# Moving source-record scatters out of the first layer's edge pass: three beside each group instead of six

## What is computed

```python
# layer 0, graph attention (8 heads of 32)
h = (x @ W).reshape(n, H, C)
e = leaky(a_src[src] + a_dst[dst])
alpha = softmax of e over the edges of each dst
out = segment_sum(h[src] * alpha, dst) + bias
x = x + layer_norm(out + x_in) * ln_w + ln_b
# layer 0, mixture: 8 experts, top 2 of a router's softmax
x = x + combine(gelu(t @ w1[e] + b1[e]) @ w2[e] + b2[e])
# layer 1, messages: need h[src], h[dst] and the projected edge attributes
```

## Time and profile before

| | |
|---|---|
| median of the runs | 7105.77 us |
| profiled execution, span | 7405.0 us (the page gives its span, and no time around it) |
| busy, PE / DVE / POOL | 67% / 56% / 49% |
| edge pass of the first layer | about 790 to 2105 us |
| end of gat, to the next block | 2105 to 2187.6 us |
| router, to the next block | 2210 to 2267.6 us |
| first mixture, to the next block | 2267.6 to 2637.2 us |

### The profile page before, as it was taken

How to read it: one execution, slowest core, us unless ns; L and a number is a source line. 1 busy time by engine, 2 the same in 40 slices (tenths; PEclk the granted TensorE clock), 3 DMA queues, 4 the chain that set the end, 5 groups by cost and what they waited for, 6 DMA issues and landing times. The chain is left out here.

```text
span 7405.0 us, 83243 instructions
## 1 busy us (share of the span) xinstructions
PE 4987.3 (67%) x21442; PEld 3487.6 (47%) x21443; DVE 4140.2 (56%) x11930; ACT 2331.7 (31%) x4546; POOL 3609.5 (49%) x3179
## 2 busy tenths in 40 slices
PE   1995477777737966667783677639994555545685
PEld 1663365555525644445552555425662323223474
DVE  9202388888874667774525777773453334433534
ACT  0332244444411223332123555533322222211132
POOL 4777677777742327771034554300007673766043
PEclk9997678877758988888856777759996677766687
DMA  2553344434412255552132222200013332333324
GB/s 52 139 141 74 84 110 112 111 108 109 108 50 69 66 87 165 160 167 64 41 85 77 69 69 68 55 15 9 13 29 93 89 93 63 90 92 88 108 77 105
DMA packets 408552, 630.27 MB, mean 85 GB/s; under 512 B 163019, under 2 KB 290119, under 8 KB 406851
## 3 DMA queue, kind: packets, MB, share of 16 engines
q0 software_dynamic: 180096, 360.11, 18.7%
q1 hardware_dynamic: 227822, 260.35, 13.3%
q10 hardware_dynamic: 308, 6.40, 0.3%
HBM read 470.99 MB, written 154.65 MB: 84 GB/s over the span
## 5 line engine op out<-in xcount | busy, mean ns | idle before, releaser
L779 POOL DMA_INDIRECT conv_rows<-rows_b,index x832 | 843.4, 1014 | 1235.4 <-SPq L2682 884.5
L811 DVE TENSOR_TENSOR acc<-acc,ps 125x257 f32 (+1 forms) x1664 | 701.4, 422 | 930.5 <-DMA acc<-slots,ffn_slot_of 348.8
L2728 PE MATMUL ps<-conv_rows,conv_weight_of 128*125 128x256 f32 x1664 | 633.0, 520 | 599.1 <-issue 297.7
L332 POOL DMA_INDIRECT records_src<-by_src_edge_stage,by_src_edge_slot x400 | 560.0, 1400 | 458.0 <-DMA by_src_edge_stage<-edge_rows 340.4
L2728 PEld LDWEIGHTS ps<-conv_rows,conv_weight_of 128*125 128x125 f32 x1664 | 367.3, 248 | 864.8 <-issue 575.8
L779 POOL DMA_INDIRECT gat_rows<-rows,index x416 | 501.9, 1207 | 256.9 <-PE ps L1089 136.2
L779 POOL DMA_INDIRECT mpnn_rows<-rows_b,index x416 | 472.9, 1137 | 305.3 <-issue 122.1
L496 POOL DMA_INDIRECT records_dst<-front_back,front_dst_addr x400 | 503.6, 1259 | 234.7 <-issue 234.7
L779 POOL DMA_INDIRECT hyp_rows<-rows,index x416 | 417.1, 1003 | 407.8 <-PE ps L2335 274.3
L2716 ACT ACTIVATE conv_weight_of<-conv_onehot_b,index 128x125 f32<-128x125 bf16 x832 | 251.5, 386 | 980.2 <-DVE conv_onehot_b L2700 797.4
L1013 ACT CAST room<-ps 125x1024 bf16<-125x1024 f32 x416 | 409.0, 1016 | 458.3 <-PE ps L1076 374.8
(11 more groups left out here) (582 smaller groups left out, 10558.5 us busy)
## 6 DMA issues: line engine op xcount, KB each, us to landing
mpnn_edge<-records_src SPq DMA_DIRECT2D x104, 512.0 KB
edge_rows<-front_edge_ring SPq DMA_DIRECT2D x100, 451.5 KB
by_src_edge_stage<-edge_rows SPq DMA_DIRECT2D x100, 451.5 KB
conv_rows<-rows_b,index POOLq DMA_INDIRECT x832
front_attr<-in_edge_attr SPq DMA_DIRECT2D x100, 112.0 KB
rows_b<-acc SPq DMA_DIRECT2D x15, 560.0 KB
second_w<-in_L_ffn_w SPq DMA_DIRECT2D x1, 8192.0 KB
slots<-mlp_y SPq DMA_DIRECT2D x56, 128.0 KB
```

Source lines behind the costliest of these rows:

```text
L332: pool.indirect_dma_start(out=self.S.records["src"], out_offset=bass.IndirectOffsetOnAxis(ap=self.addr[:, c:c + 1], axis=0), in_=self.stag ...
L779: pool.indirect_dma_start(out=rows[:, n % U, t, :], out_offset=None, in_=table, in_offset=bass.IndirectOffsetOnAxis(ap=ends[:, n * G + t:n ...
L811: dve.tensor_tensor(here, here, S.ps[0:P, t % banks, 0:width], ALU.add).then_inc(added, 1)
L2728: pe.matmul(S.ps[0:P, t, 0:D], weight_of[:, q.slot, t, :], rows[:, q.slot, t, :], start=True, stop=True).then_inc(summed, 1)
```

## The change

The same 400 columns are scattered in the same order; their division over the four places goes from 312 + 24 + 28 + 36 to 156 + 48 + 40 + 156. In the mixture SP now issues the weights of an expert first and the edge loads behind them, and the loads begin with expert 1 and not with expert 2. The rule that divides the rest over the experts gives 20, 20, 20, 24, 24, 24 and 24 columns for experts 1 to 7, where it gave 4, 4, 4, 8, 8 and 8 for experts 2 to 7.

```diff
@@ gat
-                edges.load(sp, 6 * GROUPS)
+                edges.load(sp, 3 * GROUPS)
...
-                gather_groups(pool, ends, S.rows, rows, summed, gathered, go, lambda: edges.scatter(pool, 6))
+                gather_groups(pool, ends, S.rows, rows, summed, gathered, go, lambda: edges.scatter(pool, 3))
@@ gat, the end
-                edges.load(sp, 24)
+                edges.load(sp, 48)
...
-                edges.scatter(pool, 24)
+                edges.scatter(pool, 48)
@@ expert_weights
-                    edges.load(sp, 28)
+                    edges.load(sp, 40)
...
-                    edges.scatter(pool, 28)
+                    edges.scatter(pool, 40)
@@ experts
                     if e >= 2:
                         sp.wait_ge(done[h], e // 2)
-                        columns = edges.unloaded() // (steps - e)
-                        edges.load(sp, columns - columns % SG if e + 1 < steps else edges.unloaded())
                     sp.dma_start(w1[:, h], w_first(e)).then_inc(loaded[h], 16)
                     sp.dma_start(w2[:, h], w_last(e)).then_inc(loaded[h], 16)
                     if e == 0:
                         biases()
+                    if e >= 1:
+                        columns = edges.unloaded() // (steps - e)
+                        edges.load(sp, columns - columns % SG if e + 1 < steps else edges.unloaded())
```

## The result

The changed kernel takes 7151.47 us (median of 20 runs, 7094.45 to 7161.85), the kernel before 7106.95 us (20 runs, 7042.85 to 7117.21): ratio 1.0062 [1.0042, 1.0081], 44.5 us more. The forecast was 7148 us, same within 1%.

A forecast was written before the change was run, and what follows sets the result against it. DVE was taken to pace the edge pass, POOL to end gat and router last, PE to bound the mixture. Terms +35.8 + 17.9 - 10 - 1 = +42.7 us on 7105.8 gave 7148 us, range 7090 to 7195.

The forecast's parts named there:

- End of gat, +35.8 us: End of gat: 24 more scatters follow DVE's end, POOL is last, nothing hides them; 1.49 us each, +35.8 us.
- The upper end: End of gat: +39 us if each scatter costs the 1.327 + 0.3 us of the edge pass.
- Router, +17.9 us: Router block: 12 more scatters behind DVE's end, where POOL is last, at 1.49 us each, +17.9 us.
- Mixture, 0 us: Mixture: 120 more scatters hidden beside PE's experts, POOL landing before SP's last store; 0 us.
- rival 3: Mixture's tail: scatters above 1.64 us make POOL last, at 1.9 us each +13 us; 7178 us in all; chance 20%.
- The slack: Mixture's end: POOL's scatters land about 7 us before SP's last store, with landing at about 2.7 us.
- Edge pass, -10 us at the start and -1 in pace: Edge pass: fewer scatters shorten the start's burst, middle of 0 and -20 us; the steady pace, set by DVE, hardly changes.
- POOL's wait for PE, forecast at 390 us: Edge pass: POOL's wait for PE's sums grows about 5 us a group, from 136.2 to about 390 us.
- Rival 1: Edge pass: each of 51 periods loses 0.9 us and the start 20 us, giving 7094 us; chance 14%.
- Rival 2: End of gat: all 48 scatters fit beside DVE's operations, leaving the router's term and start's gain, 7113 us; chance 6%.

The follow-up runs named there:

- e_end48: Kernel before with 48 scatters instead of 24 at the end of gat, the 24 taken out of the mixture; 7533.60 us, ratio 1.0052.
- e_best: Kernel before with 16 scatters at the end of gat, 20 beside the router, 52 in the mixture with its new load order; 7457.38 us, ratio 0.9968.
- e_router40: Kernel before with 40 instead of 28 scatters beside the router, the mixture keeping 24; 7511.63 us, ratio 1.0020.
- e_mixorder: Kernel before with only the changed kernel's order of loads in the mixture's SP queue; 7490.99 us, ratio 1.0003.
- e_combo: Changed kernel with no scatters in first three groups, 4 in other 49, 16 at gat's end, 20 beside router, 168 in mixture; 7072.43 us, ratio 0.9954.
- e_pass3: Changed kernel with 24 scatters at the end of gat and 28 beside the router again, so 192 in the mixture; 7461.51 us, ratio 0.9947.
- e_none: Changed kernel with no scatters in the edge pass, 24 at the end of gat, 28 beside the router, 348 in the mixture; 7321.14 us.
- b_again: Kernel before with only an empty line added, for a second profile; 7492.18 us, ratio 1.0001.
- a_again: Changed kernel with only an empty line added, on the second chip; 7508.53 us, ratio 1.0037 to the kernel before.
- e_split: Changed kernel with each of five large DVE operations at the end of gat cut into 25 of 125x256; 7137.46 us, ratio 1.0045 to the kernel before.
- e_nofirst4: e_mixorder without scatters in the first four groups, 60 columns in the mixture; 7462.48 us, ratio 0.9963 to the kernel before.

## Why the prediction was right

**End of gat, +35.8 us.** Measured +35.4 in the changed kernel and +35.7 alone (e_end48). The reading that carried it was who ends last: POOL, 7 us behind DVE (10.3 us counted to the next block's start, e_best), so that each scatter added counts in full at 1.49 us. The upper end (+39, at the pace of the edge pass) was not needed.

**Router, +17.9 us.** +17.0, and +17.4 alone (e_router40). Right by the same reading.

**Mixture, 0 us.** -0.4 us, and e_mixorder shows that the order of SP's queue is free. POOL's pace over the last 50 issues was (2630.04 - 2554.43)/50 = 1.51 us, under the 1.64 of rival 3. The slack was 3.9 us, where the forecast had 7: landing took 4.2 us and not 2.7, and POOL's DRAIN of 2.8 us was not in the forecast at all; on the other side SP closed 4.7 us behind the start of its last store, to which the forecast had counted. That the slack is small but real is bracketed by 168 columns (e_combo, no loss) and 192 (e_pass3, 4 to 8 us lost, POOL last).

**Edge pass, -10 us at the start and -1 in pace.** Measured -9.0 by the second scaling and -0.8 behind it. The size was right by luck: its reason was not. The forecast took the middle between a stall that ends with the burst and one that does not, from a profile in which ACT waited 14.21 us for something outside the trace, and DVE 20.26 us for ACT. In the profiles at 7105 us, ACT has no such wait. The gain there is plain order in POOL's queue: the gathers of groups 2 to 4 stand behind fewer scatters. It is smaller than the 17.9 us of scatters taken out, because the second scaling cannot come much earlier: it is 64.9 us behind the first gather in the changed kernel, and still 62.4 with no scatter at all (e_none; 62.6 in e_combo). POOL's wait for PE, forecast at 390 us, was 321.9: it started from 97.3 on this chip and not from 136.2.

**Rival 1** (the pass gains) does not hold where the kernel runs at 7105 us: even with no scatters the period falls by 0.11 us only. It holds in part on the first two chips: start -13.5 us, period from the second scaling 24.49 to 24.05, 35.6 us in all (b_again to a_again; 10.0 us and 24.55 to 24.05 against e_mixorder), and the time grew by 25 us and not by 44. It was weighed at 0.9 us a group; half of that was there.

**Rival 2** (hidden at the end of gat) is excluded by e_end48. By the rule of the Trainium skill (SBUF — State Buffer, "Who interferes with whom") that it rested on, `tensor_tensor` of two SBUF inputs would not hold POOL's descriptor generation. The trace of the changed kernel disagrees once more (11.41 us beside L1155), and e_split narrows it: a single long operation holds it to its end, and 25 short ones of the same kind let most scatters through but hold one to the end of the run in five cases of six.

**Rival 3** (the mixture's tail) did not come at 156 columns. At 192 (e_pass3) POOL is last in the mixture, though not by a slower scatter: 28 columns of the last expert stand in front of the paddings, the last padding is issued later, and its landing took 6.6 us.

## What to carry to other kernels

Work taken out of a loop whose pace another engine sets bought only what it held up at the loop's start (at 7105 us; on the other two chips the period fell by 0.44 to 0.52 us as well). Put down behind the last work of a short block it costs its full time, here 1.49 us a scatter. Before moving work, list for each block which engine ends last and by how much: with that list the better division was the opposite one in the short blocks. Count to where the engine closes the block, landing and DRAIN included, and not to its last issue. In the first iterations of a pipeline look at what stands in the issuing engine's queue ahead of the next group's loads.

## What the runs showed of the hardware

- The same kernel takes some 7105 us on one chip and 7490 on two others (7110.8 and 7489.1 us in the two profiled executions compared here), with the median of DVE's scaling at 2284 ns in both. 74 of the 378 us lie ahead of the end of the edge pass; where the rest lies was not looked into. In that pass ACT waited 21 times, 123.0 us, for a releaser outside the trace, and on the third chip never. What it waits for stays open; with three scatters a group it was 40.5 us, but with none in the first four groups alone (e_nofirst4) still 122.1.
- One long operation of DVE on two SBUF tiles holds a scatter until 1.07 us behind its end (11.41 us for 1.19; 1.41 beside the 25 short ones of e_split). In five of six runs of 25 short ones a single scatter is held to 1.06 or 1.07 us behind the run's end (3.39 to 5.57 us). Beside 25 BATCH_NORM_STATS2 and 25 TENSOR_SCALAR of 125x256 (changed kernel, 2088 to 2109 us) none took over 1.2 us.
- POOL's DRAIN at the end of the mixture took 2.83 us (changed kernel, e_pass3), beside 1.02 us of DVE's and 0.01 of SP's. Its last scatter landed 4.2 us (changed kernel) and 6.6 us (e_pass3) behind its end.
